# One reduction for the overall maximum, and smaller last pieces, at the end of a gated block

## What is computed

```python
xq = _act_fake_quant(x, clip_x[0])
gate = jnp.einsum('bsh,ih->bsi', xq, _weight_fake_quant(w_gate))
up = jnp.einsum('bsh,ih->bsi', xq, _weight_fake_quant(w_up))
h = _act_fake_quant(jax.nn.silu(gate) * up, clip_down[0])
return jnp.einsum('bsi,hi->bsh', h, _weight_fake_quant(w_down))
# _act_fake_quant: scale = sigmoid(clip) * max(|x|) / 127; round, clip to -128..127, times scale
# and around it: x = x + tanh(g_ffn[0]) * ffn(layernorm(x))
```

## Time and profile before

| what | value |
|---|---|
| timed runs | 106.43, 106.78, 106.75 us, median 106.75 |
| profiled execution, its own time | 106.31 us |
| its span | 104.5 us |
| PE busy | 96.9 us (93%) |
| DVE busy | 80.6 us (77%) |
| granted TensorE clock | 1.0 in all slices |

### The profile page before, as it was taken

One profiled execution on the slowest core, in us unless ns is written; L12 is line 12 of the kernel. 1 busy time (PEld: TensorE's weight loads), 2 busy tenths in 40 slices (PEclk: granted clock), 3 DMA queues, 4 the chain that ended last, 5 costly groups with the idle time before them and its releaser, 6 DMA issues.

```text
span 104.5 us, 1739 instructions
## 1 busy us (share of the span) xinstructions
PE 96.9 (93%) x562; PEld 75.1 (72%) x564; DVE 80.6 (77%) x210; ACT 66.1 (63%) x125; POOL 43.6 (42%) x78
## 2 busy tenths in 40 slices
PE   7799999999999999999999987999999697899990
PEld 2268988988889898897878975444444386889970
DVE  0544296497998999597597979559999998879991
ACT  0421071657972755636738978789888989799800
POOL 6030335047083583508517594055696560350000
PEclk9999999999999999999999999999999999999999
DMA  2999999999354010010985500000000000005555
GB/s 51 333 371 336 376 422 419 419 407 401 138 6 44 0 45 9 23 34 0 150 154 116 110 0 0 0 6 3 0 0 0 0 0 0 0 6 192 209 201 201
DMA packets 11176, 13.54 MB, mean 130 GB/s; under 512 B 6432, under 2 KB 7712, under 8 KB 11168
## 3 DMA queue, kind: packets, MB, share of 16 engines
q1 hardware_dynamic: 10304, 12.39, 37.9%
q10 hardware_dynamic: 864, 1.05, 3.2%
HBM read 10.09 MB, written 2.10 MB: 117 GB/s over the span
## 4 chain that ended last, share of the span: by engine, by line
PE 47%; DVE 20%; DMA 16%; POOL 5%; issue 4%; ACT 3%; SPq 1%; DVEq 0%; POOLq 0%
PE ps L465 9%; DVE hmax L1100 9%; PE ps L686 9%; DMA spread<-rstd 8%; PE ps L503 5%; PE ps L485 5%; DMA r_wide<-spread 5%; DMA wk_sb<-in_wk 4%; DVE shared L1095 4%; PE ps L635 2%; POOL shared L436 2%; PE ps L523 2%; PE ps L540 2%; PE ps L691 2%; PE ps L516 2%
## 5 line engine op out<-in xcount | busy, mean ns | idle before, releaser
L635 PE MATMUL ps<-xq,wguT 128*128 128x512 bf16 x78 | 17.2, 379 | 0.7 <-DVE xq L1075 0.6
L436 POOL TENSOR_TENSOR shared<-up_sb,silu 128x1024 f32<-128x1024 f32 x5 | 11.8, 2366 | 9.5 <-ACT up_sb L830 9.5
L635 PEld LDWEIGHTS ps<-xq,wguT 128*128 128x128 bf16 x80 | 7.8, 98 | 9.8 <-issue 0.6
L465 PE MATMUL ps<-wvT,shared 128*128 128x256 f32 x56 | 13.3, 381 | 0.0
L485 PE MATMUL ps<-shared,a_sb 128*128 128x256 f32 x56 | 13.2, 379 | 0.0
L1100 DVE TENSOR_REDUCE hmax<-shared 128x1 f32<-128x2048 f32 (+1 forms) x6 | 12.7, 2109 | 0.6
L825 ACT ACTIVATE silu<-ps,gu_scale 128x1024 f32<-128x1024 f32 x10 | 11.2, 1115 | 2.1 <-PE ps L635 2.1
L503 PEld LDWEIGHTS ps<-uT,shared 128*128 128x128 f32 x64 | 10.7, 190 | 2.2 <-DVE uT L892 1.0
L503 PE MATMUL ps<-uT,shared 128*128 128x256 f32 (+1 forms) x64 | 12.0, 330 | 0.2 <-DVE uT L892 0.2
L465 PEld LDWEIGHTS ps<-wvT,shared 128*128 128x128 f32 x56 | 10.6, 190 | 1.8 <-DMA shared<-in_xc 0.4
L686 PE MATMUL ps<-hq,wdT 128*128 128x256 bf16 x80 | 10.6, 273 | 0.3 <-DVE hq L1135 0.3
(11 more groups left out here) (120 smaller groups left out, 188.4 us busy)
## 6 DMA issues: line engine op xcount, KB each, us to landing
shared<-in_xc SPq DMA_DIRECT2D x6, 512.0 KB, 10.8
out<-xn SPq DMA_DIRECT2D x7, 256.0 KB, 2.0
xs<-in_x SPq DMA_DIRECT2D x3, 512.0 KB, 8.4
shared<-in_wgu SPq DMA_DIRECT2D x3, 512.0 KB, 7.8
wd<-in_wd SPq DMA_DIRECT2D x1, 896.0 KB, 11.8
shared<-in_xc SPq DMA_DIRECT2D x3, 256.0 KB, 6.9
xs<-in_x ACTq DMA_DIRECT2D x2, 256.0 KB, 5.4
r_wide<-spread SPq DMA_DIRECT2D x4, 128.0 KB, 4.7
```

What stands on the lines that cost most here:

```text
L436: nc.gpsimd.tensor_tensor(hid[:, 2 * i + 1, :], up_sb[i % 2][:], silu1[i % 2][:], ALU.mult).then_inc(hid_done[1], 1)
L465: last = nc.tensor.matmul(values_bank(b, k), ctxT(b)[:, e, k * P:(k + 1) * P], weights[:, e, :], start=(e == 0), stop=(e == KT - 1))
L635: last = nc.tensor.matmul(bank(4 * half + 2 * g + c), wguT[:, i, g, k, :], xq[:, k, col:col + CH], start=(k == 0), stop=(k == KT - 1))
```

## The change

Two edits.

1. `hmax` has no tile of its own any more. It is five columns (`FULL`) directly behind the eleventh slot of `hid`, in `shared`. The last reduction goes over slot 9, slot 10 and those five columns at once, 2053 numbers, and writes `col_max` directly.

2. Step 6 has its tiles in two banks (5 and 0), and DVE finishes each when it is done. In step 7 the tile `t = 0` is as before (bank 6); the tile `t = 1` is computed as two pieces of 128 tokens, in banks 7 and 1, each with its own increment of `down_done` and its own finishing instruction. The output of the tile is sent as before in one transfer, once both pieces are finished.

```diff
-        shared = sb("shared", [P, (2 * FULL + 1) * HALF])
+        shared = sb("shared", [P, (2 * FULL + 1) * HALF + FULL])
...
+        hmax = shared[:, (2 * FULL + 1) * HALF:]
...
+            if c == STEPS - 2:
+                return ps[:, 5 if t == 0 else 0, 0:2 * P]
             return bank2(c - 1)[:, t, :]
+
+        def last_half(half):
+
+            return ps[:, 7 if half == 0 else 1, 0:P]
...
-                sp.wait_ge(res_done, STEPS + t)
+                sp.wait_ge(res_done, STEPS + 2 * t)
...
+                    if c == STEPS - 2:
+                        pe.wait_ge(res_done, 2)
                 else:
-                    pe.wait_ge(res_done, 1)
-                for t in range(KT):
-                    down_products(c, t, range(SLOTS))
+                    pe.wait_ge(res_done, 3)
+                down_products(c, 0, range(SLOTS))
+                if c < STEPS - 1:
+                    down_products(c, 1, range(SLOTS))
+            for half in range(2):
+                for i in range(FULL):
+                    nc.tensor.matmul(last_half(half), wdT[:, i, P:D],
+                                     hq[(STEPS - 1) % HQ_BUFS][:, 2 * i + half, :], start=(i == 0), stop=False)
+                nc.tensor.matmul(last_half(half), wdT[:, FULL + half, P:D],
+                                 hq[(STEPS - 1) % HQ_BUFS][:, 2 * FULL, :], start=False, stop=True).then_inc(down_done, 1)
...
-            largest_hidden(FULL, 2 * FULL - 1, 2)
-
-            dve.wait_ge(hmax_done, FULL + 1)
-            nc.vector.tensor_reduce(col_max[:, 1:2], hmax[:], AX.X, ALU.max).then_inc(col_max_done, 1)
+            dve.wait_ge(hmax_done, FULL)
+            nc.vector.tensor_reduce(col_max[:, 1:2], shared[:, (2 * FULL - 1) * HALF:], AX.X, ALU.max,
+                                    apply_absolute_value=True).then_inc(col_max_done, 1)
...
-            finish_step(STEPS - 2)
+            dve.wait_ge(x1T_ready, STEPS - 1)
+            for t in range(KT):
+                dve.wait_ge(down_done, KT * (STEPS - 2) + t + 1)
+                last = finish(STEPS - 2, t)
+            last.then_inc(res_done, 1)
             dve.wait_ge(x1T_ready, STEPS)
-            for t in range(KT):
-                dve.wait_ge(down_done, KT * (STEPS - 1) + t + 1)
-                finish(STEPS - 1, t).then_inc(res_done, 1)
+            dve.wait_ge(down_done, KT * (STEPS - 1) + 1)
+            finish(STEPS - 1, 0).then_inc(res_done, 1)
+            for half in range(2):
+                tokens = slice(half * P, (half + 1) * P)
+                dve.wait_ge(down_done, KT * (STEPS - 1) + half + 2)
+                nc.vector.scalar_tensor_tensor(out=x1T[:, STEPS - 1, 1, tokens], in0=last_half(half),
+                                               scalar=out_scale[:, 1:2], in1=x1T[:, STEPS - 1, 1, tokens], op0=ALU.mult,
+                                               op1=ALU.add).then_inc(res_done, 1)
```

More of the change, by code:

```diff
@@ L68, in gated_block @@
         wgu = shared[:, XC:XC + SLOTS * 2 * D].rearrange("p (s n d) -> p s n d", s=SLOTS, n=2)
-        hid = shared[:].rearrange("p (s n) -> p s n", n=HALF)
+        hid = shared[:, 0:(2 * FULL + 1) * HALF].rearrange("p (s n) -> p s n", n=HALF)
+        hmax = shared[:, (2 * FULL + 1) * HALF:]
         wq_sb = sb("wq_sb", [P, KT, D])
@@ L142, in gated_block @@
         up_sb = [sb(f"up_sb{p}", [P, HALF]) for p in range(2)]
-        hmax = sb("hmax", [P, FULL + 1])
         out_scale = sb("out_scale", [P, KT])
```

## The result

The changed kernel took 105.91 us (median of 6 runs, 105.67 to 105.97), the kernel before in the same comparison 106.52 (6 runs). The ratio is 0.9942, 95% interval 0.9924 to 0.9960: 0.61 us faster, between 0.43 and 0.81. The profiled execution took 105.68 us, its span is 103.9 us.

What follows compares the result with a forecast made beforehand. Bounds taken: PE in the down stage with DVE close behind, DVE alone in the second barrier. Terms 0.185 + 0.155 = 0.34 us, so 106.75 - 0.34 = 106.41, predicted 106.4 us, range 105.9 to 107.0.

Steps and rivals of the forecast that it cites:

- Edit 1: Second barrier: dropping the small reduction over `hmax` starts PE's spreading and all behind it 0.185 us earlier.
- Edit 2 at DVE: Tail: DVE's last instruction starts when it did but is shorter, so DVE ends 0.13 us earlier.
- the hand-over takes 0.03 us: Tail, step 7's first tile: DVE starts finishing 0.03 us after PE ends it, at 101.05 us.
- The size taken for edit 2: End of kernel: 0.155 us earlier, chosen between bounds of 0.13 (DVE's gain) and 0.25 (all that step 6 gains).
- My own sum for the queue: Output transfers: step 6 issued earlier, so the queue is through at 103.44 us, 0.2 us earlier.
- the queue still ends last, by a little: Output transfers after the change: queue through at 103.44 us, the last transfer by itself at 103.33.
- Added waits on PE: PE's new waits for finished steps before steps 6 and 7: long met, costing nothing.
- Paced products: Rival, last tile: weight loads pace 128-column products; at 0.098 us each, 0.0 us gained in sum; chance 0.11.
- Moved tiles: Rival, start of kernel: tiles shifted 32 bytes slow transfers; at 10%, 0.55 us slower in sum, 107.3 us; chance 0.11.
- Only one of the two counts: Rival, barrier or tail: one edit's gain is swallowed; 0.17 us faster, 106.58 us; chance 0.13.
- One sign that I had named for being wrong: First part of the kernel: the span before 85 us changing by more than 0.2 us would refute the prediction.
- one that I had named for being right: Tail: DVE's seven finishing instructions would come 0.40 us apart at most, without an idle gap from the last clip.

Runs made afterwards that it cites:

- one_wait: The changed kernel with DVE's wait for the last `x1T` copy moved ahead of step 6's finishing; ratio 0.9939 to the kernel before.
- step6_only: The kernel before with only step 6's tiles in two banks, each finished when done, and the last tile whole; ratio 0.9963.
- short_products: The kernel before with down's products of slots 1 to 4 in every tile split into two of 128 columns; ratio 1.0021.
- moved_tiles: The kernel before with `hmax` declared directly behind `shared`, so tiles between its new and old places start 32 bytes later; ratio 1.0008.
- after_again: The changed kernel run once more, unaltered, against the kernel before; ratio 0.9963, 0.39 us faster.
- pieces_only: The kernel before with only the last tile computed and finished in two pieces, step 6 as before; ratio 0.9984.

## Why the prediction was right, step by step

- **Faster by a little, at the edge of what can be told.** Right in sign. Forecast 0.34 us; the stages show 0.20 + 0.21 = 0.41, two comparisons 0.61 and 0.39. That the median, 105.91, lies inside the range, 0.01 us above its lower edge (105.9), is in part luck. The three runs I had gave 106.75 for the kernel before, six gave 106.52, and 0.23 us of the distance to my 106.4 was that; another 0.2 us of the first comparison is in no term of the sum and stands in no stage that the edits touch.
- **Edit 1, 0.185 us.** Right. From the start of the last reduction to PE's spreading it measures 2.62 - 2.44 = 0.18 us; between the two spreadings it is 0.20 in every kernel that has the edit and at most 0.01 in every one that hasn't. The last 0.01 to 0.02 us lies ahead of the reduction, and nothing here explains it. Nothing else bound the spreading, and what follows moved along: the first product of down comes 2.31 us behind the second spreading in both kernels (90.82 - 88.51 and 90.41 - 88.10).
- **Edit 2 at DVE, 0.13 us.** Measured 0.08 (second spreading to DVE's end, 13.69 to 13.61). The step that failed is "the hand-over takes 0.03 us": with a wait for `x1T` next to the one for PE it took 0.09, and one_wait, without it, took 0.02. The other starts came as worked out: pieces 0.26 us apart, 0.34 us long. The upper bound of this term, 0.55 us later, doesn't follow from its rival either: at 0.116 us for each product the sum gives 0.59.
- **The size taken for edit 2, 0.155 us.** Mis-sized: 0.21. My own sum for the queue moved its end by 0.24 us (103.68 to 103.44), and I took a value near DVE's gain all the same. step6_only shows the queue's part by itself: 0.15 us with DVE's end unchanged. Behind that the sentence "the queue still ends last, by a little" doesn't hold for step6_only, whose traffic thins out ahead of the last transfer; there the last issue decides, and the pieces bring their 0.06 us through it. In the changed kernel the two are about level: its last transfer lands as soon after its issue as step6_only's. The time in the queue was too long in my sum as well, 0.2 us; without it the last transfer ends 0.13 us sooner after its issue. So the mechanism was right, earlier traffic and an earlier last issue, and the choice between them was a guess: both count, one after the other.
- **Added waits on PE, nothing.** Right: PE's last product ends 13.17 us behind the second spreading before and 13.18 after.
- **Paced products, 0.11.** Refuted for this kernel: ten in a row at 0.056 us in short_products, and the twelve of the changed kernel at 0.34 us for six.
- **Moved tiles, 0.11.** Refuted at the size that would have decided, over 0.66 us: moved_tiles is at most 0.42 us slower. As a gain of 0.2 us it is not excluded by the timed runs of moved_tiles, but the first parts of the traces show none.
- **Only one of the two counts, 0.13.** Refuted by the stages: 0.20 us and 0.21 us in the kernels with one edit, and the same two in the changed kernel.

One sign that I had named for being wrong did appear, and one that I had named for being right didn't. The part before 85 us changed by over 0.2 us (0.21 at the first spreading); after_again, the same kernel, has 61.30 us there, longer than before, so I hold it to be chance. And DVE's finishing instructions are not 0.40 us apart at most: before step 7's first tile it is 0.58 us (100.13 to 100.71). My own sum had 0.49 there, so that sign contradicted it.

What stays open: the timed ratios of the tail's kernels (0.39, 0.47 us) lie above what their traces show (0.15, 0.21). Their intervals are about 0.2 to 0.3 us to each side, and step6_only's lower end, 0.20, misses its trace's number, as the lower end of the first comparison, 0.43, just misses 0.41. Chance in the first part would do it; no run shows that it did.

## What to carry to other kernels

Where a tail ends in transfers, ask first when their traffic starts, and only then how long the last instruction is: finishing step 6's tiles earlier brought 0.15 us with the last instruction unmoved, and a shorter last instruction nothing alone and 0.06 us behind it. When executions differ by more than the change, cut the traces at an instruction that both kernels have, and compare stage by stage: here two stages repeat within 0.04 us while the first moves by 1.6. A wait that is long met can still cost when it stands between the last producer and its consumer, here 0.07 us at that instruction and 0.03 at the end; put it ahead of an earlier instruction.

## What the runs showed of the hardware

Products of 128 columns, each behind a load of 128 x 128 weights in bf16, followed one another at 0.056 us over ten in a row (short_products) and over twelve (the changed kernel, where each slot's weights are new) at full clock (1.00), though each weight load is recorded as 98 ns long. The Trainium skill, TensorE: Matmul & The Clock Gate, section Back-to-back issue gap, has about 56 ns for the isolated gap at that size, and this stream agrees with that figure, not with the sustained one. A second wait on DVE ahead of an instruction, for a semaphore long met, made it start 0.07 us later. The last transfer of 128 KB landed 1.9 us after its issue where the traffic ahead of it ran on without a hole (before, pieces_only), and 1.7 us after it where step 6's transfer had been issued 0.27 us earlier (step6_only, the changed kernel).
